# Maximum of four of sixteen heads applied as the bias of ScalarE's exponential, one head at a time

## What is computed

```python
scores = einsum('bhqd,bhkd->bhqk', Q, K) / sqrt(8)
scores = where(mask == 0, -1e9, scores)      # not in l2x
attn   = softmax(scores, axis=-1)
out    = einsum('bhqk,bhkd->bhqd', attn, V)
x      = layernorm(x + out @ Wo + bo)        # l0a: without Wo
```

## Time and profile before

| | us |
|---|---|
| median of 3 runs | 1494.11 |
| lowest and highest | 1493.06, 1494.60 |
| the profiled execution | 1494.57 |
| its span, first to last instruction | 1492.4 |
| stretch of `l0a` | 17.7 to 92 |
| stretch of `l1x` | 788 to 865 |
| stretch of `l2x` | 1096 to 1170 |
| stretch of `l3a` | 1248 to 1335 |
| stretch of `l3x` | 1340 to 1440 |

### The profile page before, as it was taken

How to read it: one execution, slowest core, us unless ns; L and a number is a source line. 1 busy time by engine, 2 the same in 40 slices (tenths; PEclk the granted TensorE clock), 3 DMA queues, 4 the chain that set the end, 5 groups by cost and what they waited for, 6 DMA issues and landing times. The chain is left out here.

```text
span 1492.4 us, 18333 instructions
## 1 busy us (share of the span) xinstructions
PE 927.2 (62%) x6190; PEld 610.4 (41%) x6190; DVE 1049.9 (70%) x2464; ACT 605.1 (41%) x1211; POOL 126.8 (8%) x259
## 2 busy tenths in 40 slices
PE   4844244345787204245997835899868616867877
PEld 2522122222455103235874522666545304644643
DVE  4867898984565698984336856799659586966842
ACT  2644555550443404244114614665127321644632
POOL 0110000101000000000011130000011021020100
PEclk9975667666898656677998957899869756988967
DMA  5000000001123600001000000000000000000000
GB/s 184 2 1 0 0 0 0 0 0 42 51 67 88 262 0 1 1 0 50 1 1 1 1 0 0 1 0 1 0 1 2 1 0 0 2 1 1 1 1 14
DMA packets 25382, 29.17 MB, mean 20 GB/s; under 512 B 657, under 2 KB 22033, under 8 KB 24274
## 3 DMA queue, kind: packets, MB, share of 16 engines
q1 hardware_dynamic: 25298, 28.09, 5.7%
HBM read 18.65 MB, written 9.44 MB: 19 GB/s over the span
## 5 line engine op out<-in xcount | busy, mean ns | idle before, releaser
L1910 DVE TENSOR_TENSOR_SCAN l2a_hs<-l2a_decay,l2a_b_ps 128x512 f32<-128x512 f32 x64 | 78.0, 1221 | 14.3 <-ACT l2a_decay L1840 6.1
L1765 PEld LDWEIGHTS l2a_b_ps<-l2a_diag,l2a_uT 128*128 128x128 f32 x512 | 64.1, 191 | 39.3 <-issue 38.0
L2323 PE MATMUL l1w_mem_ps<-l1a_rows,l1w_post 128*128 128x64 f32 x16 | 4.3, 363 | 110.6 <-DVE l1a_rows L2464 110.6
L1765 PE MATMUL l2a_b_ps<-l2a_diag,l2a_uT 128*128 128x128 f32 x512 | 69.9, 280 | 1.9 <-DVE l2a_hs L1910 1.7
L1773 PE MATMUL l2a_acc_ps<-l2a_hc,pack 128*128 128x512 f32 x128 | 65.5, 595 | 1.0 <-DVE l2a_hc L1921 1.0
L2437 DVE MATCH_REPLACE8 l1w_minus<-l1w_low,l1w_minus 128x129 f32<-128x129 f32 (+39 forms) x264 | 64.5, 263 | 0.0
L2431 DVE MAX8 l1w_low<-l1w_minus 128x8 f32<-128x129 f32 (+37 forms) x332 | 59.7, 261 | 0.4
L833 PE MATMUL l0x_scores<-pack,l0x_prob 128*128 128x128 f32 x128 | 25.4, 363 | 54.6 <-ACT l0x_prob L968 54.6
L2351 ACT ACTIVATE l1w_score<-l1w_mix_ps 128x264 f32<-128x264 f32 (+7 forms) x29 | 11.4, 447 | 107.2 <-DVE l1a_rows L2464 92.1
L1840 ACT ACTIVATE l2a_decay<-l2a_dt,pack 128x1016 f32<-128x1016 f32 x32 | 36.4, 1141 | 45.5 <-DVE l2a_hs L1910 45.5
L2330 PE MATMUL l1w_at_ps<-l1w_post,l1a_rows 128*128 128x128 f32 x256 | 42.9, 343 | 13.4 <-ACT l1a_rows L2374 13.4
(11 more groups left out here) (595 smaller groups left out, 2764.5 us busy)
## 6 DMA issues: line engine op xcount, KB each, us to landing
scores_dram<-l1p_dots SPq DMA_DIRECT2D x8, 1056.0 KB, 6.4
l1a_rows<-scores_dram SPq DMA_DIRECT2D x8, 1056.0 KB, 13.0
pack<-in_pack SPq DMA_DIRECT2D x1, 697.5 KB, 9.5
pack<-in_pack SPq DMA_DIRECT2D x2, 321.5 KB, 6.7
pack<-in_pack SPq DMA_DIRECT2D x1, 612.0 KB, 11.4
pack<-in_pack SPq DMA_DIRECT2D x1, 576.0 KB, 10.4
pack<-in_pack SPq DMA_DIRECT2D x1, 514.0 KB, 8.0
x_tok<-in_x SPq DMA_DIRECT2D x1, 512.0 KB, 4.3
```

The source lines that it names most:

```text
L1765: mm = nc.tensor.matmul(bx_ps(n)[:, j * S:(j + 1) * S], uT[:, c, b, :], diag[:, s % 2, b, :], start=True, stop=True)
L1910: nc.vector.tensor_tensor_scan(hs[:, n % 2, :], decay[:, k % 2, batches, :].rearrange("p b t -> p (b t)"), bx_ps(n), 0.0, ALU.mult, ALU.ad ...
```

## The change

In half 0, heads 0 to 3 are treated as before. For heads 4 to 7 DVE no longer subtracts the maximum: ACT reads the scores from PSUM and adds the negated maximum as a [128,1] bias, one instruction a head. So that the bias can be added after the scale, the factor 1/sqrt(8) is moved into `q` and the exponential's scale is 1 (`exp_scale`). With rotary positions the scale stays in the exponential, and DVE scales the four negated maxima into `shift` instead. Half 1 is treated as before. The reduces now give negated maxima, `mx` has two buffers, and `score` waits for `prob_set` too, because ACT now reads the score banks.

```diff
+    exp_scale = scale if rope else 1.0
...
-        mx = sc.sb("mx", [128, 2, HALF])
+        mx = [sc.sb(f"mx{n}", [128, 2, HALF]) for n in range(2)]
+        shift = [sc.sb(f"shift{n}", [128, HH]) for n in range(2)] if rope else [m[:, 0, HH:HALF] for m in mx]
...
                     if bias_mask is not None:
+                        after(pe, prob_set, 2 * b - 1)
                         for g in range(HH):
                             nc.tensor.matmul(bank(g), cm.ident_bf[:], bcast_mid(bias_mask, HH), start=True, stop=False)
+                    after(pe, prob_set, 2 * b - 1)
...
                 def exponential(b, half):
                     act.wait_ge(diff_set, 2 * b + half + 1)
-                    nc.scalar.activation(prob[b % 2][:, half, :, :], prob[b % 2][:, half, :, :], ACT.Exp,
-                                         scale=scale).then_inc(prob_set, 1)
+                    if half:
+                        nc.scalar.activation(prob[b % 2][:, half, :, :], prob[b % 2][:, half, :, :], ACT.Exp,
+                                             scale=exp_scale).then_inc(prob_set, 1)
+                        return
+                    nc.scalar.activation(prob[b % 2][:, 0, 0:HH, :], prob[b % 2][:, 0, 0:HH, :], ACT.Exp, scale=exp_scale)
+                    if rope:
+                        act.wait_ge(shift_set, b + 1)
+                    for h in range(HH):
+                        ins = nc.scalar.activation(prob[b % 2][:, 0, HH + h, :], scores[:, 0, HH + h, :], ACT.Exp,
+                                                   scale=exp_scale, bias=shift[b % 2][:, h:h + 1])
+                    ins.then_inc(prob_set, 1)
...
-                        nc.vector.tensor_scalar(q[b % 2][:], qk_ps[:, 0, :], w("bq"), None, ALU.add)
+                        nc.vector.tensor_scalar(q[b % 2][:], qk_ps[:, 0, :], w("bq"), scale, ALU.add, ALU.mult)
...
-                        nc.vector.tensor_copy(q[b % 2][:], qk_ps[:, 0, :])
+                        nc.vector.tensor_scalar(q[b % 2][:], qk_ps[:, 0, :], scale, None, ALU.mult)
...
                 def maximum(b, half):
-                    s, m = scores[:, half, :, :], mx[:, half, :]
+                    s, m = scores[:, half, :, :], mx[b % 2][:, half, :]
+                    part = HALF if half else HH
                     per = 2 if prefix else 1
                     dve.wait_ge(scores_mm, 2 * b + half + 1)
-                    nc.vector.tensor_reduce(m, s, AX.X, ALU.max).then_inc(max_set, 1)
+                    after(dve, turn_mm, turn(b - 2, half, 1) + 1)
+                    nc.vector.tensor_reduce(m, s, AX.X, ALU.max, negate=True).then_inc(max_set, 1)
...
-                    after(dve, turn_mm, turn(b - 2, half, 1) + 1)
-                    nc.vector.tensor_tensor(prob[b % 2][:, half, :, :], s, bcast_last(m, S),
-                                            ALU.subtract).then_inc(diff_set, 1)
+                    if rope and half == 0:
+                        nc.vector.tensor_scalar(shift[b % 2][:], m[:, HH:HALF], scale, None, ALU.mult).then_inc(shift_set, 1)
+                    nc.vector.tensor_tensor(prob[b % 2][:, half, 0:part, :], s[:, 0:part, :], bcast_last(m[:, 0:part], S),
+                                            ALU.add).then_inc(diff_set, 1)
```

More of the change, by code:

```diff
@@ L351, in attention @@
                                 "sums_set", "sums_mm", "recip_set", "o_set", "oT_mm", "oT_set", "y_mm"))
+        shift_set = sc.sem("shift_set")
         if prefix:
@@ L537, in exponential_prefix @@
                         act.wait_ge(pre_diff, b + 1)
-                        nc.scalar.activation(ppre[b % 2][:], ppre[b % 2][:], ACT.Exp, scale=scale).then_inc(pre_set, 1)
+                        nc.scalar.activation(ppre[b % 2][:], ppre[b % 2][:], ACT.Exp, scale=exp_scale).then_inc(pre_set, 1)
                 def copy_v(b):
@@ L627, in prefix_maximum @@
                         dve.wait_ge(pre_copied, b + 1)
-                        nc.vector.tensor_reduce(mpre[:], pre[:], AX.X, ALU.max).then_inc(pre_max, 1)
+                        nc.vector.tensor_reduce(mpre[:], pre[:], AX.X, ALU.max, negate=True).then_inc(pre_max, 1)
                 def maximum(b, half):
-                    s, m = scores[:, half, :, :], mx[:, half, :]
+                    s, m = scores[:, half, :, :], mx[b % 2][:, half, :]
+                    part = HALF if half else HH
                     per = 2 if prefix else 1
                     dve.wait_ge(scores_mm, 2 * b + half + 1)
-                    nc.vector.tensor_reduce(m, s, AX.X, ALU.max).then_inc(max_set, 1)
+                    after(dve, turn_mm, turn(b - 2, half, 1) + 1)
+                    nc.vector.tensor_reduce(m, s, AX.X, ALU.max, negate=True).then_inc(max_set, 1)
                     dve.wait_ge(max_set, per * (2 * b + half) + 1)
@@ L637, in maximum @@
                         dve.wait_ge(pre_max, b + 1)
-                        nc.vector.tensor_tensor(m, m, mpre[:, HALF * half:HALF * half + HALF], ALU.max) \
+                        nc.vector.tensor_tensor(m, m, mpre[:, HALF * half:HALF * half + HALF], ALU.min) \
                             .then_inc(max_set, 1)
                         dve.wait_ge(max_set, per * (2 * b + half) + 2)
-                    after(dve, turn_mm, turn(b - 2, half, 1) + 1)
-                    nc.vector.tensor_tensor(prob[b % 2][:, half, :, :], s, bcast_last(m, S),
-                                            ALU.subtract).then_inc(diff_set, 1)
+                    if rope and half == 0:
+                        nc.vector.tensor_scalar(shift[b % 2][:], m[:, HH:HALF], scale, None, ALU.mult).then_inc(shift_set, 1)
+                    nc.vector.tensor_tensor(prob[b % 2][:, half, 0:part, :], s[:, 0:part, :], bcast_last(m[:, 0:part], S),
+                                            ALU.add).then_inc(diff_set, 1)
                 def prefix_difference(b):
@@ L648, in prefix_difference @@
                         nc.vector.tensor_tensor(ppre[b % 2][:].rearrange("p a h m -> p (a h) m"), pre[:],
-                                                bcast_last(mx[:].rearrange("p a h -> p (a h)"), PRE),
-                                                ALU.subtract).then_inc(pre_diff, 1)
+                                                bcast_last(mx[b % 2][:].rearrange("p a h -> p (a h)"), PRE),
+                                                ALU.add).then_inc(pre_diff, 1)
                 def divide(b):
```

## The result

| | before | after |
|---|---|---|
| median of 6 runs, us | 1494.13 | 1505.67 |
| lowest to highest | 1492.59 to 1494.60 | 1503.14 to 1514.38 |
| the profiled execution | 1494.57 | 1503.14 |
| its span | 1492.4 | 1500.8 |

The ratio is 1.0086, with a 95% interval of 1.0062 to 1.0111. By the medians the change makes the kernel slower by 11.5 us. The forecast had +19.0 (1513.1, range 1507 to 1519). The direction held, and so did the ring through `turn_ps` in `l0a`, `l1x`, `l2x` and `l3x`. The size did not, and neither did the picture of `l3a` and of the start and end of `l3x`.

What follows compares the result with a forecast made beforehand. The prediction took a PE-ACT ring through `turn_ps` to bound most stages, with DVE limiting `l2x` and `l3a`. Terms 5.0 + 5.0 + 4.1 + 3.8 + 1.1 = 19.0 us on 1494.1 gave 1513.1 us, range 1507 to 1519.

Steps and rivals of the forecast that it cites:

- the ring through `turn_ps`: PE and ACT wait on each other through one bank; half 0's exponential lies on it, period 7.84 us in `l1x`.
- the term of `l3x`: In `l3x`, seven batches pay 0.73 - 0.17 = 0.56 us each, less 0.1: +3.8 us.
- x = 0.73: What ACT pays per batch, in us, for splitting half 0's exponential: 1.68 against 0.95.
- (a): DVE's difference of half 0 shrinks from 1024 elements to 512, saving 0.54 us a batch.
- (b): On ACT, half 0's exponential becomes one of 512 elements and four of 128 at 0.29 us, costing 0.73 a batch.
- (c): In `l3a` DVE adds the tiny `shift`, 0.20 us with a gap, so DVE saves 0.34 there.
- (d): PE's new waits on `prob_set` cost nothing, since transposes ahead of the score already wait for that count.
- (e): The scale on `q` is off the ring or rides on existing instructions; two `mx` buffers and the moved wait are free.
- the slack: In `l3x`, PE's transposes could start 0.17 us earlier than they do, at 1393.64 instead of 1393.81.
- 1: Rival: DVE sets the pace everywhere and ACT's work hides, saving 20.0 us, 1474.1; chance 0.03.
- 2: Rival: the four small exponentials pipeline like the value copy, 0.21 us extra a batch, +3.0 us, 1497; chance 0.06.
- 3: Rival: PE's longer pauses cost it its full clock, one stage 22 us, 1535; chance 0.05.

Runs made afterwards that it cites:

- `only_l3x`: The kernel before with the change made in `l3x` alone, the other four stages as before: 1490.38 us, ratio 0.9993.
- `act_only`: The kernel before with only ACT's exponential of half 0 cut into one of 512 elements and four of 128 from SBUF, DVE unaltered: 1514.65 us, ratio 1.0137.
- `one_exp`: The changed kernel with one 512-element exponential in place of the four small ones, using one head's maximum for all four: 1484.93 us, ratio 0.9943.
- `all_but_l3x`: The kernel before with the change made in `l0a`, `l1x`, `l2x` and `l3a`, and `l3x` as before: 1506.01 us, ratio 1.0099.
- `stat`: The changed kernel with DVE's statistics in `l3a` moved between the q and k parts of the rotary copy: 1502.19 us, ratio 1.0080.
- `after_late`: The changed kernel with twelve extra DVE multiplications at the start of `l0a`, a delay of about 9 us: 1512.29 us.

## Why the prediction was wrong in size

Two steps failed. The larger is the term of `l3x`: the forecast charged +3.8 us with the stretches at its start and behind its end unchanged, and `only_l3x` measured -1 us. The other is the price of a small exponential, x = 0.73 where the rows show 0.57. Without the first the forecast would stand near 1508, without both near 1505.

The forecast's terms beside the two traces of each kernel. The marks are the first exponential of half 0 of each stage, which the forecast has 0.54 us earlier against its stage. The fourth column is an estimate: the measured intervals from the second on, and for the first interval and the end of each stage the forecast's own sum with x = 0.57 (good to some 0.3 us).

| from, to | forecast | measured, twice | with measured periods |
|---|---|---|---|
| start, `l0a` | -0.5 | -0.4, -0.6 | -0.5 |
| `l0a`, `l1x` | 5.0 | 3.3, 3.4 | 3.9 |
| `l1x`, `l2x` | 5.0 | 3.2, 5.4 | 4.0 |
| `l2x`, `l3a` | 4.1 | 4.1, 1.3 | 3.2 |
| `l3a`, `l3x` | 1.1 | 0.1, 3.0 | 1.6 |
| `l3x`, end | 4.3 | -1.8, -1.8 | 4.0 |
| sum | 19.0 | 8.4, 10.8 | 16.2 |

The traced executions of after are 1 to 2.5 us under its medians, so the medians' 11.5 to 13 agree with these sums. The single rows in the middle differ by up to 3 us between the two pairs of traces, since such starts and ends of stages differ from execution to execution.

- **(a) DVE saves 0.54 a batch: right** (0.69 at 833.53, as the earlier trace rows had it), and worth nothing in `l0a`, `l1x` and `l3x` in this order of ACT, as forecast.
- **(b) x = 0.73 was mis-sized: 0.57**, and 0.61 on the period, since the transposes now start 0.78 us after the copy (836.44 to 837.22) where it was 0.74. The step that failed is "0.008 less, so 0.287": I took the difference of two durations for the difference of the times from start to start. The row compared (L555) reads PSUM as the new instruction does, but it is alone; the eight in a chain read SBUF. From start to start the small exponentials take 0.25 in after and 0.29 from SBUF in `act_only`, 0.04 less. By the table this is worth about 3 us outside `l3a`, and on its own would have put the forecast at about 1510.
- **(c) The shift was charged 0.20 and takes 0.07** (1321.95 to 1322.02); DVE saves 0.46 in `l3a`, as `one_exp` shows, not 0.34. It is lost nevertheless. The step by which DVE's cycle falls to 8.55 and "the ring's own" rises to 8.57 "and sets the pace by a hair" left out the second ring, 8.87. Periods of 8.89 did not become 8.57 but stayed; the term rose from 1.1 to 1.6.
- **(d), (e): right** as far as the rows show: the masks at 838.58, behind the new wait for `prob_set`, start without idle time of PE.
- **`l2x`**: the period is 7.77 where 7.87 was forecast, and DVE's gap 0.83 for "about 1.0", but at the statistics. The ring at 7.14 + 0.61 = 7.75 was read rightly. **`l3x`**: 10.16 for 10.2; 10.16 - 0.61 = 9.55 makes the slack 0.12 for my 0.17.
- **The main miss is the last row of the table ahead of the sum, 6 us.** The forecast put "3 to 4" us for "the starts of stages, whose slow-clock stretches may shift" into the range, and centred it on no change. It thought of the starts alone. From the last exponential of `l3x` to the end it had about +0.6 where the traces show -3.4 and -3.5, and for the first interval about +0.4 where they show -1.4 and -1.3. `only_l3x` prices it: 0.49 us a batch longer and no slower in all. The other side agrees: `all_but_l3x` is 14.7 us slower (12 to 18), where the forecast without `l3x` was 15.2 and the sum with the measured periods is 12.7; its interval can't tell these two apart, so the mis-sized x is shown by the rows, not by the time. Why the clock comes back sooner in `l3x` is open.
- **Rivals.** 1 fell with `one_exp`. 2 has the right price for another form; with 0.25 the truth lies nearer to the forecast. 3 fell at its size: in the first trace of after the clock is 1.00 from the second to the last exponential of `l0a`, `l1x`, `l3a` and `l3x`, and in the rows of `l2x` above, with PE at 80 to 85%; what remains of it is the one stretch of 3.4 us in `l3a` in the second trace. The rule of the Trainium skill, page "TensorE: Matmul & The Clock Gate", section "A second HAM failure mode: psum-queue depth-cycling", was named beside it; longer pauses of PE between groups (0.29 to 0.90 us) did not make the clock swing from batch to batch here. The clock did act on the result, but mainly at the start and behind the end of `l3x`, and in favour of the change.

## What to carry to other kernels

Before you hand work from a full engine to a half-empty one, look at whether the receiving engine starts its work without an idle moment and the next engine waits for its end: there it is latency that is bought, not throughput. Let the first consumer wait for the first part only, and put the rest behind the copies that others wait for; that turned +12 us into -8 with the same instructions. When the limit falls, ask for the next ring through all engines (here 0.19 us away), and read the pace of chained small instructions from a chain with the same source and operands, not from durations.

## What the runs showed of the hardware

- An ACTIVATE of 128 elements takes 0.16 us from start to start from PSUM with numbers as operands; each [128,1] scale or bias adds 0.09, a source in SBUF 0.04 (five forms, 0.16 to 0.385). 128 elements more add 0.11 (0.40 for 256, 0.29 for 128).
- Around `l3x` the stretches in which TensorE is granted 0.50 depend on the work in that stage: with delays of 0, 4 and 9 us ahead, its first interval in the kernel before was 11.31 to 11.33 each time. Between the two forms of `l3x` the stretch at its start was 10.2 or 6.8 us long (in `stat` it began earlier and was longer), and those behind its last exponential 27 to 31 us in sum or 14 (17 in `stat`, 21 in `after_late`); that outweighs half a microsecond on each of eight batches.
- Other such stretches differ between executions of one kernel: a first interval by 0.7 to 1.4 us (`l2x` 8.45 and 7.76, `l3a` 8.32 and 9.70), a last one by 1.5. One trace therefore can't price a change of 1 us in a short stage.
